# V's bias as two rows on TensorE, V a group ahead of u, and 22 transposes of the identity, in the first stage of a decoder layer

## What is computed

```python
scaled = hidden_states / (input_norm + 1e-09)      # hidden_states = layernorm(x)
q = jnp.einsum('bsh,oh->bso', scaled, Wq) + bq
v = jnp.einsum('bsh,oh->bso', scaled, Wv) + bv
tq = jnp.einsum('bsh,hk->bsk', q, anomaly_matrix)
scores = jnp.einsum('bsh,bth->bst', q, tq) / jnp.sqrt(jnp.float32(HIDDEN))
probs = jax.nn.softmax(scores, axis=-1)
ctx = jnp.einsum('bst,bth->bsh', probs, v)
return ctx * input_norm
```

## Time and profile before

| | |
|---|---|
| runs, median (lowest to highest) | 826.67 us (826.08 to 827.56), 3 runs |
| the profiled execution: its time, its span | 824.5 us, 822.3 us |
| busy TensorE, VectorE, ScalarE, GpSimd (share of the span) | 753.7 us (92%), 629.5 (77%), 456.1 (55%), 165.8 (20%) |
| mean granted TensorE clock | 0.968 of full speed |

### The profile page before, as it was taken

The page is one execution under the profiler, slowest core; times in us unless marked ns, Lnnn a source line. Parts: engine busy times, 40 slices in busy tenths (PEclk is TensorE's granted clock), DMA queues, the critical chain, the costliest instruction groups (busy, mean ns, idle before and its releaser), DMA issues. The chain is left out here.

```text
span 822.3 us, 19916 instructions
## 1 busy us (share of the span) xinstructions
PE 753.7 (92%) x6231; PEld 668.3 (81%) x6232; DVE 629.5 (77%) x1614; ACT 456.1 (55%) x924; POOL 165.8 (20%) x255
## 2 busy tenths in 40 slices
PE   4867978999999999999999999999997769999996
PEld 4766867888888888888888888888896658999996
DVE  5782835798888988889889898898886855777773
ACT  2444625766666666666666666666664712443342
POOL 3110022203123032130320312303122011222221
PEclk9888989999999999999999999999999969999999
DMA  6044074133131231321313303133167281111110
GB/s 218 5 139 142 0 271 141 57 110 108 40 128 67 77 106 38 132 89 49 106 40 130 106 32 111 58 108 106 38 225 305 98 326 28 36 41 39 41 32 16
DMA packets 51147, 80.95 MB, mean 98 GB/s; under 512 B 4894, under 2 KB 29216, under 8 KB 50976
## 3 DMA queue, kind: packets, MB, share of 16 engines
q1 hardware_dynamic: 49232, 75.63, 27.5%
q0 software_dynamic: 1872, 4.76, 1.6%
HBM read 45.60 MB, written 35.18 MB: 98 GB/s over the span
## 5 line engine op out<-in xcount | busy, mean ns | idle before, releaser
L1185 ACT ACTIVATE ps_cross<-flip 128x512 f16<-128x512 f32 (+1 forms) x256 | 124.8, 515 | 104.7 <-PE flip L897 83.5
L1409 DVE TENSOR_TENSOR ps_cross<-flip,ps_cross 128x512 f16<-128x512 f32 (+1 forms) x256 | 145.0, 584 | 29.9 <-ACT ps_cross L1185 29.0
L1370 ACT ACTIVATE exp_cross<-exp_cross,xneg 128x1024 f32<-128x1024 f32 (+1 forms) x128 | 122.7, 960 | 27.3 <-DVE xneg L1599 27.3
L897 PE MATMUL flip<-ident,exp_cross 128*128 128x128 f32 (+1 forms) x832 | 130.0, 279 | 6.7 <-DVE ps_cross L1409 3.6
L886 PE MATMUL scores<-keys_cross,qt 128*128 128x402 f32 x512 | 126.4, 369 | 3.6 <-ACT exp_self L1359 1.9
L897 PEld LDWEIGHTS flip<-ident,exp_cross 128*128 128x128 f32 (+1 forms) x832 | 94.0, 141 | 15.1 <-DVE ps_cross L1409 5.1
L739 PE MATMUL scores<-keys_self,u_tile 128*128 128x512 f32 x384 | 102.2, 403 | 4.1 <-issue 2.2
L908 PE MATMUL cross_out<-vals_cross,ps_cross 128*128 128x128 f16 (+1 forms) x832 | 100.7, 222 | 0.3 <-DVE ps_cross L1409 0.2
L910 PE MATMUL cross_out<-vals_cross,ps_cross 128*128 128x64 f16 (+1 forms) x832 | 94.0, 194 | 0.0
L873 PE MATMUL flip<-vals_self,ps_self 128*128 128x256 f16 x768 | 93.7, 276 | 0.0
L908 PEld LDWEIGHTS cross_out<-vals_cross,ps_cross 128*128 128x128 f16 (+1 forms) x832 | 75.4, 100 | 20.9 <-issue 14.7
(11 more groups left out here) (225 smaller groups left out, 1215.8 us busy)
## 6 DMA issues: line engine op xcount, KB each, us to landing
rows_dram<-pads SPq DMA_DIRECT2D x17, 520.0 KB, 4.0
w_piece<-W SPq DMA_DIRECT2D x32, 256.0 KB, 2.9
w_dram<-w_high SPq DMA_DIRECT2D x32, 256.0 KB, 2.3
w_dram<-w_piece SPq DMA_DIRECT2D x32, 256.0 KB, 2.7
w1s<-w_dram SPq DMA_DIRECT2D x8, 1024.0 KB, 12.6
w2s<-w_dram SPq DMA_DIRECT2D x8, 1024.0 KB, 12.5
u_dram<-u_out SPq DMA_DIRECT2D x4, 1024.0 KB, 5.9
u_tile<-u_dram SPq DMA_DIRECT2D x16, 256.0 KB, 2.7
```

Of the source, the lines that this page charges most:

```text
L897: tr = pe.transpose(flip[0:rows, bank(use), n * P:(n + 1) * P], exp_cross[:, h % 2, m * P:m * P + rows], ident[:, :])
L1185: return act.activation(out, in_, ACT.Copy, **kw)
L1370: act.activation(exp_cross[:, h % 2, cols], exp_cross[:, h % 2, cols], ACT.Exp, bias=xneg[:, h % 2, 1:2], scale=-1.0, accum_out=xden[:, ha ...
L1409: return dve.tensor_tensor(out, full, hi, ALU.subtract)
```

## The change

- **V's bias on TensorE.** bv is split into two float32r rows on one partition (`bv_parts`); each tile of V begins with two matmuls of a row of ones by these rows, and `three` goes on adding to them. The 16 bias adds of VectorE are gone, and V's parts are made straight from PSUM, two tiles at a time (`v_hi` on ScalarE, `v_lo` on VectorE), 8 of each in place of 16.
- **V ahead.** TensorE makes u of a group, then V of the next group, then the flips of the group after; u goes to `scores[0]` and `scores[1]`. On VectorE and ScalarE the order follows: V's parts first, then the flips' copies, then u. The split of the cross weights moves one group later on VectorE, and the row scaling stands behind u instead of ahead of it.
- **The start.** The bound's sum comes right behind the transposes of Wq, the one-column products with bq behind the first flips, the second group's statistics behind the first group's splits.
- **Transposes of the identity**, into a bank that V(0) writes later: 12 ahead of Wq's transposes, 10 behind the bound's sum.

```diff
@@ tensor
+        for n in range(12):
+            pe.transpose(scores[:, 2, 0:P], ident[:, :], ident[:, :])
         pe.wait_ge(self_w_loaded, 48)
...
         tr.then_inc(wq_flipped, 1)
+        pe.wait_ge(bound_step, 2)
+        pe.matmul(scores[:, 3, 0:1], ones[:, :], bound16[:, :], start=True, stop=True).then_inc(bound_summed, 1)
+        for n in range(10):
+            pe.transpose(scores[:, 2, 0:P], ident[:, :], ident[:, :])
         flip_x_pro(0)
+        pe.wait_ge(biases_loaded, 64)
+        for o in range(C):
+            for c in range(C):
+                mm = pe.matmul(cross_out[:, 8 + o:9 + o], w_raw[:, 2, c, o * P:(o + 1) * P], bq_col[:, c:c + 1],
+                               start=(c == 0), stop=(c == C - 1))
+        mm.then_inc(bias_mixed, 1)
         pe.wait_ge(self_w_lo, 2)
...
                 if g == 0:
                     pe.wait_ge(self_w_lo, 3)
+                    pe.wait_ge(bv_parts_set, 2)
+                    pe.wait_ge(bound_step, 3)
                 pe.wait_ge(pro_xt_lo, C * (g + 1))
                 if g and n % 2 == 0:
-                    pe.wait_ge(pro_v_biased, 4 * (g - 1) + n + 2)
...
+                    pe.wait_ge(pro_v_lo, 2 * (g - 1) + n // 2 + 1)
+                out = scores[:, 2 + n // 2, (n % 2) * D:(n % 2 + 1) * D]
+                for part in range(2):
+                    pe.matmul(out, one_row[:, :], bv_parts[:, part, :], start=(part == 0), stop=False)
...
-        self_u(0)
-        for g in range(1, GROUPS):
-            self_v(g)
+        for g in range(GROUPS):
+            self_u(g)
             if g < GROUPS - 1:
-                flip_x_pro(g + 1)
-            self_u(g)
-
+                self_v(g + 1)
+            if g < GROUPS - 2:
+                flip_x_pro(g + 2)
@@ scalar
+        def v_hi(g):
+            for n in range(2):
+                act.wait_ge(pro_v_ready, 4 * g + 2 * n + 2)
+                act.wait_ge(self_scale_step, 2)
+                act.activation(vals_self[:, 4 * g + 2 * n:4 * g + 2 * n + 2, 0, :],
+                               scores[:, 2 + n, :].rearrange("p (m d) -> p m d", m=2), ACT.Copy,
+                               scale=self_scale[:, 0:1]).then_inc(pro_v_hi, 1)
+
         xt_hi_pro(0)
+        act.wait_ge(biases_loaded, 64)
+        copy(bv_parts[:, 0, :], bv_row[0:1, :]).then_inc(bv_hi, 1)
...
         for g in range(GROUPS):
+            if g:
+                v_hi(g)
             if g < GROUPS - 1:
                 xt_hi_pro(g + 1)
-            for n in range(4):
-                act.wait_ge(pro_v_biased, 4 * g + n + 1)
...
             u_hi(g)
@@ vector
         statistics_pro(0)
-        statistics_pro(1)
+        dve.wait_ge(self_w_loaded, 48)
...
+        dve.wait_ge(bound_summed, 1)
+        dve.tensor_copy(v_bound[:, 1:2], scores[:, 3, 0:1]).then_inc(bound_step, 1)
+        dve.wait_ge(biases_loaded, 64)
+        dve.wait_ge(bv_hi, 1)
+        low(bv_parts[:, 1, :], bv_row[0:1, :], bv_parts[:, 0, :].bitcast(F32)).then_inc(bv_parts_set, 1)
+        statistics_pro(1)
...
         for g in range(GROUPS):
+            if g:
+                v_lo(g)
             if g < GROUPS - 1:
                 xt_lo_pro(g + 1)
...
             if g < GROUPS - 2:
                 statistics_pro(g + 2)
...
+            u_lo(g)
             if g < GROUPS - 2:
                 scale_rows(g + 2)
-            u_lo(g)
-
-            if g == 0:
+
+            if g == 1:
                 for dup in range(2):
...
-            if g == 1:
+            if g == 2:
                 for n, w in ((1, wv_cross), (2, wq_cross), (3, wo_cross)):
@@ gpsimd
         for g in range(4):
-            if g == 2:
+            if g == 1:
                 pool.wait_ge(bound_step, 3)
```

More of the change, by code:

```diff
@@ L163, in emit @@
     mixed_bias = sb("mixed_bias", [P, 2, C], F32, pro)
+    bv_parts = sb("bv_parts", [1, 2, D], F32R, pro)
+    one_row = sb("one_row", [1, P], F32R, pro)
     u_out = sb("u_out", [P, 4, 2 * C, P], F32R, pro)
@@ L267, in emit @@
     pro_v_ready = sem("pro_v_ready")
-    pro_v_biased = sem("pro_v_biased")
+    bv_hi = sem("bv_hi")
+    bv_parts_set = sem("bv_parts_set")
     pro_v_hi = sem("pro_v_hi")
@@ L751, in self_u @@
                     pe.wait_ge(u_lo_ready, C * (g - 1) + o + 1)
-                out = self_out if o == 0 else cross_out
-                three(out[:, :], lambda a, c: mixed[:, 1, a, c, o * P:(o + 1) * P],
+                three(scores[:, o, :], lambda a, c: mixed[:, 1, a, c, o * P:(o + 1) * P],
                       lambda b, c: keys_self[:, b, c, g * 512:(g + 1) * 512]).then_inc(pro_u_ready, 1)
@@ L785, in self_v @@
                     pe.wait_ge(self_w_lo, 3)
+                    pe.wait_ge(bv_parts_set, 2)
+                    pe.wait_ge(bound_step, 3)
                 pe.wait_ge(pro_xt_lo, C * (g + 1))
                 if g and n % 2 == 0:
-                    pe.wait_ge(pro_v_biased, 4 * (g - 1) + n + 2)
-                three(scores[:, 2 + n // 2, (n % 2) * D:(n % 2 + 1) * D],
-                      lambda a, c: keys_self[:, a, c, (4 * g + n) * P:(4 * g + n + 1) * P],
-                      lambda b, c: w_self[:, 1, b, c, :]).then_inc(pro_v_ready, 1)
+                    pe.wait_ge(pro_v_lo, 2 * (g - 1) + n // 2 + 1)
+                out = scores[:, 2 + n // 2, (n % 2) * D:(n % 2 + 1) * D]
+                for part in range(2):
+                    pe.matmul(out, one_row[:, :], bv_parts[:, part, :], start=(part == 0), stop=False)
+                three(out, lambda a, c: keys_self[:, a, c, (4 * g + n) * P:(4 * g + n + 1) * P],
+                      lambda b, c: w_self[:, 1, b, c, :], first=False).then_inc(pro_v_ready, 1)
         self_v(0)
@@ L798, in _ @@
         mm.then_inc(mixed_ready, 1)
[L799 to L806, removed]
         flip_x_pro(1)
         pe.wait_ge(mixed_bias_set, 1)
-        pe.wait_ge(bound_step, 3)
         for o in range(C):
@@ L1197, in u_hi @@
                     act.wait_ge(u_stored, 16 * g)
-                out = self_out if o == 0 else cross_out
                 act.wait_ge(mixed_bias_set, 2)
-                act.activation(u_out[:, :, o, :], out[:, :].rearrange("p (t s) -> p t s", t=4), ACT.Identity,
+                act.activation(u_out[:, :, o, :], scores[:, o, :].rearrange("p (t s) -> p t s", t=4), ACT.Identity,
                                bias=mixed_bias[:, 1, o:o + 1]).then_inc(u_hi_ready, 1)
@@ L1447, in u_lo @@
                 dve.wait_ge(u_hi_ready, C * g + o + 1)
-                out = self_out if o == 0 else cross_out
-                dve.scalar_tensor_tensor(out=u_out[:, :, C + o, :], in0=out[:, :].rearrange("p (t s) -> p t s", t=4),
+                dve.scalar_tensor_tensor(out=u_out[:, :, C + o, :], in0=scores[:, o, :].rearrange("p (t s) -> p t s", t=4),
                                          scalar=mixed_bias[:, 1, o:o + 1], in1=u_out[:, :, o, :].bitcast(F32), op0=ALU.add,
@@ L1453, in _, with v_lo @@
         dve.memset(ctx_t[:, :, :, M:MP].bitcast(F32), 0.0).then_inc(v_scale_step, 1)
-        statistics_pro(0)
-        statistics_pro(1)
+        dve.memset(one_row[:, :].bitcast(F32), 1.0).then_inc(bv_parts_set, 1)
+        def v_lo(g):
+            for n in range(2):
+                dve.wait_ge(pro_v_hi, 2 * g + n + 1)
+                dve.scalar_tensor_tensor(out=vals_self[:, 4 * g + 2 * n:4 * g + 2 * n + 2, 1, :],
+                                         in0=scores[:, 2 + n, :].rearrange("p (m d) -> p m d", m=2), scalar=self_scale[:, 0:1],
+                                         in1=vals_self[:, 4 * g + 2 * n:4 * g + 2 * n + 2, 0, :], op0=ALU.mult,
+                                         op1=ALU.subtract).then_inc(pro_v_lo, 1)
+        statistics_pro(0)
+        dve.wait_ge(self_w_loaded, 48)
+        dve.tensor_tensor_reduce(v_tmp[:, :, :].rearrange("p c n -> p (c n)"), w_raw[:, 1, :, :].rearrange("p c n -> p (c n)"),
+                                 w_raw[:, 1, :, :].rearrange("p c n -> p (c n)"), 1.0, 0.0, ALU.mult, ALU.add,
+                                 v_bound[:, 0:1]).then_inc(bound_step, 1)
+        dve.wait_ge(bound_step, 1)
+        dve.tensor_scalar(bound16[:, :], v_bound[:, 0:1], 1.02, None, ALU.mult).then_inc(bound_step, 1)
         scale_rows(0)
```

66 lines of the change are left out of this document (21 added, 45 removed).

## The result

The changed kernel takes 830.0 us (median of 8 runs, 824.18 to 832.12) against 826.38 for the kernel before (8 runs). The ratio is 1.0044, interval 1.0027 to 1.0061: slower by 0.44%, 3.6 us. That is above the range of the prediction, which had forecast a gain. The profiled execution has a span of 827.9 us, mean granted clock 0.960 (before 822.3 and 0.968).

The account below looks back on a forecast made before the run. Bound: the work before u's first store, then three rounds through its single buffer. First store -2.95, round 1 +0.03, round 2 +1.57 sum to -1.35 us on the median 826.67: forecast 825.3 us, range 821.9 to 828.6.

Parts of the forecast that it names:

- the step on V(0): First group's V on TensorE: bias products priced by their columns, clock rising near 21.1, end at 23.9 (23.2 to 24.6).
- The start at 14.66 behind the small loads: TensorE's one-column bq products, now ahead of the first mixing product, wait for wg, the last small load, landing at 14.66.
- The lower level at the mixing product: TensorE's first mixing product runs at the lower clock, taking 2.72 us and ending at 19.16.
- the upper-level rival: The 22 identity transposes raise TensorE's clock and it holds over the gap: 2.95 us more gain, 822.4; chance 0.20.
- u(0) at the upper level: First group's u on TensorE takes 2.95 us at the higher clock, from 28.25 to 31.2.
- The slower rival: TensorE's clock falls in the one-column block; u(0) takes about 5.4 us instead of 2.95: 827.8, up to 828.6; chance 0.20.
- From u(0)'s end to the first store: ScalarE's u_hi and weight copies, then the context's parts: first store of u at 36.85, 2.95 us earlier than 39.80.
- The rounds: Store-to-store cycles of u's single buffer: first 12.90 against 12.87 us, second 11.27 against 9.70, third unchanged.
- the forecast's sum of -1.35: Whole chain up to the fourth u: -2.95 at the first store, +0.03 and +1.57 in the first two cycles.
- the 828.6 of a late V(0): Top of the range: u(0) at the lower clock, with the first group's V also ending late.

## Why the prediction was wrong

**What failed is the step on V(0).** It said: a one-row product is priced by its columns, 0.227 us at the lower level, and the clock rises 3.1 to 6.1 us after dense work begins, so V(0) ends at 23.9. Both halves were wrong, and the second weighs more. V(0) ended at 27.80 and took 9.07 us where the sum had 4.8. At the lower level some 2.4 us of that are price: a pair takes 0.72 us and the six behind it 1.58, where over 128 rows they take 0.43 and 1.28. The other 1.9 us over the sum, and 1.1 us more in the second mixing product (2.56 for 1.48) and 0.6 in the flips behind it (1.52 for 0.91), are the clock: from 15.89 on, unbroken work with the one-row products in it did not raise it until about 31.7, where the same products over 128 rows did within some 5.8 us. The rows behind "3.1 to 6.1 us" were all of work over 128 rows, and I carried them over to work that was not.

**By its other steps.**
- The start at 14.66 behind the small loads: 14.37. The lower level at the mixing product: right, 2.84 us (2.72 in the sum), the clock having fallen at 14.6, just behind the wait. The 0.20 for the upper-level rival (the first in the list, though the lines on the transposes call it the second) was not idle: with the wait short or gone it came (1.52 and 1.53 us for the mixing product in two experiments).
- u(0) at the upper level: right in the number, 2.92 us (2.95), but by another way. The sum had a clock that was up from 21.1 on and outlasted the one-column products; here it rose at 31.7, just ahead of them (31.88). That it can outlast them, the run with the bq products moved shows (u(0) 2.94 us, the clock up since before). The slower rival, u(0) at the lower level, did not happen; what it named, a clock that stays down and costs because u no longer waits for V, did happen earlier, in V(0) and the second mixing product.
- From u(0)'s end to the first store 5.70 us (5.65). The rounds 12.87, 11.27 (12.90, 11.27). These terms stood.
- So the first store was due at 36.85 and went out at 42.21: 5.4 us late, all of it ahead of u(0). With it, the forecast's sum of -1.35 becomes +4.0; the chain lost 3.88 at the fourth u, the medians 3.6. (Two of its sums are off by 0.1 us, the middle of 19.5 and 22.5 and the 828.6 of a late V(0); nothing hangs on them.)

**What the change did.** Taking the bias adds off VectorE and V ahead of u shortened what follows u(0), as meant: from its end to the first store it is 5.70 us, 8.4 before. Moving the three weights' splits into round 2 cost 1.57 us there. But V(0) had always stood ahead of u(0) on TensorE, and it now carries the one-row products, with the wait for the small loads ahead of that, on a path that had slack before: `u_hi(0)` waited for V's bias adds until 33.02, and u(0) had been done 1.6 us earlier.

## What to carry to other kernels

Before adding a bias by a matmul of one row, ask which level TensorE's clock has there; the same product over 128 rows (a constant 1/128 against the bias on all partitions) was cheaper here at both levels, and the clock rose with it. Transposes that warm TensorE showed a gain clear of the noise here only where the wait for the small loads stood behind the first dense product; so look for the waiting step, and move it there first. And where one buffer is stored round by round, put into the store's wait everything that the next round does not need, but check which engine then feeds the round.

## What was not expected of the hardware

- Two matmuls of one row by 256 columns took 0.72 us at the lower level and 0.43 at the upper, the same over 128 rows 0.43 and 0.23; the six matmuls of 128 rows behind them took 1.58 and 0.90 instead of 1.28 and 0.72. Why the shorter operand is slower was not tried.
- With two such products in eight, TensorE's clock did not rise from 0.50 in the 9.07 us of V(0), nor in most of the 4.1 us of products and flips behind it. In all four profiled executions in which such a V(0) ran at the lower level (9.07, 9.07, 9.07 and 8.81 us) the clock rose only behind it; in the four in which V(0) began at the lower level without one-row products (the kernel before, with and without the transposes, V without its bias, and 128 rows without transposes) it rose inside V(0). Where the clock was up it stayed up through 5.20 us of the same mix in one experiment, and in another it fell 0.25 us into it, 1.3 us behind a wait of 1.15. Whether the rows themselves or the slower matmuls behind them keep it down stays open.
